# Residual sums, expert sums and gate biases accumulated in PSUM by TensorE, in a fused eight-stage metaformer kernel

## The reference, cut to what matters

```
x = x + L0_conv(ln(x))   # 7x7 neighbourhood attention
t = t + L0_ffn(ln(t))    # top 2 of 8 experts, weights softmax of the router
x = x + L1_conv(ln(x))   # 3x3 convolution by L1 distances, minus L2 distances
t = t + L1_ffn(ln(t))    # expert choice: 16 experts take 8 tokens of each image
x = x + L2_conv(ln(x))   # two deformable convolutions with batch norm between
t = t + L2_ffn(ln(t))    # top 2 of 8 experts again
x = x + L3_conv(ln(x))   # full attention, 4 heads, relative positions
t = t + L3_ffn(ln(t))    # expert choice again
```

## Time and profile before

| | us |
|---|---|
| median of 3 runs | 466.93 (466.06 to 466.94) |
| profiled execution, its own time | 465.76 |
| span of its profile, first to last instruction | 464.0 |
| PE busy / DVE busy / ACT busy / POOL busy | 399.2 / 365.1 / 272.8 / 167.3 |

### The profile page before, as it was taken

The page is one execution under the profiler, slowest core; times in us unless marked ns, Lnnn a source line. Parts: engine busy times, 40 slices in busy tenths (PEclk is TensorE's granted clock), DMA queues, the critical chain, the costliest instruction groups (busy, mean ns, idle before and its releaser), DMA issues.

```text
span 464.0 us, 10053 instructions
## 1 busy us (share of the span) xinstructions
PE 399.2 (86%) x4050; PEld 279.2 (60%) x4050; DVE 365.1 (79%) x731; ACT 272.8 (59%) x458; POOL 167.3 (36%) x158
## 2 busy tenths in 40 slices
PE   6988989989887797999878879998788996998775
PEld 5867952223246665666667556666588874554664
DVE  4778888899982577999995779999966866898521
ACT  2742177999905267887742678887412236898240
POOL 5000500000000037899982378999850500000000
PEclk9999999999999799999999999999999996999895
...
DMA packets 1630, 9.89 MB, mean 21 GB/s; under 512 B 208, under 2 KB 976, under 8 KB 1104
## 3 DMA queue, kind: packets, MB, share of 16 engines
...
...
## 4 chain that ended last, share of the span: by engine, by line
DVE 32%; PE 23%; ACT 9%; issue 6%; POOL 2%; DVEq 0%; ACTq 0%; POOLq 0%
DVE SMT L931 8%; DVE PRD L912 6%; DVE wb L912 6%; PE bank L1312 6%; ACT RINGS L605 3%; PE bank L1422 3%; PE bank L1052 2%; PE bank L1402 2%; DVE SMT L923 2%; ACT RINGS L622 1%; PE bank L1197 1%; PE bank L1295 1%; PE bank L1189 1%; ACT RINGS L547 1%; POOL HY L340 1%
## 5 line engine op out<-in xcount | busy, mean ns | idle before, releaser
L1312 PE MATMUL bank<-VB,RINGS 64*128 64x144 f32 x1152 | 95.5, 299 | 18.0 <-DVE wb L912 7.3
L1312 PEld LDWEIGHTS bank<-VB,RINGS 64*128 64x128 f32 x1152 | 76.3, 186 | 43.6 <-issue 19.6
L1052 PE MATMUL bank<-cst 128*128 128x128 f32 x650 | 79.4, 282 | 0.0
L1052 PEld LDWEIGHTS bank<-cst 128*128 128x128 f32 x650 | 78.0, 199 | 0.6
L340 POOL TENSOR_TENSOR HY<-OM,cst 128x324 f32<-128x324 f32 x32 | 23.3, 748 | 121.1 <-DVE LXA L898 121.1
L912 DVE TENSOR_TENSOR PRD<-bank,HY 128x864 f32<-128x864 f32 x48 | 50.3, 1051 | 4.7 <-PE bank L1312 4.1
L912 DVE TENSOR_TENSOR wb<-bank,HY 128x864 f32<-128x864 f32 x48 | 50.4, 1051 | 4.0 <-PE bank L1312 3.4
L547 ACT ACTIVATE RINGS<-bank,cst 128x768 f32<-128x768 f32 x48 | 42.8, 891 | 17.7 <-PE bank L1295 17.6
L550 ACT ACTIVATE RINGS<-RINGS,cst 128x768 f32<-128x768 f32 x48 | 44.9, 936 | 1.6
L1248 PE MATMUL bank<-RINGS,cst 128*32 128x512 f32 x336 | 40.7, 594 | 5.6 <-DVE RINGS L836 2.0
L501 ACT ACTIVATE RINGS<-PRD,wb 128x2048 f32<-128x2048 f32 (+1 forms) x21 | 39.5, 1920 | 5.3 <-PE bank L1248 4.3
(11 more groups left out here) (256 smaller groups left out, 701.2 us busy)
## 6 DMA issues: line engine op xcount, KB each, us to landing
...
```

What stands on the lines that cost most here:

```text
L1052: pe.matmul(bk[:, 0:P], ident, ident, start=True, stop=True)
L1312: ins = pe.matmul(view(bank[q % 2 * 2 + gp], k3 * NR, [[3 * NR, 2 * CG], [1, NR]]), view(HX, b % 2 * HXN + (3 * t + k3) * NPIX + half * P, ...
```

## The change

The two halves of every block's output now land in PSUM banks that already hold the residual: PE multiplies the identity by XT into the bank (`residual`, start without stop), and the block's last matmuls add to it. DVE's `norm` reads the sum from that bank (NORM_SRC names it); ACT copies the bank to XT after its square roots. Only norm 1 still reads XT. In `norm`, mean and centring are one instruction that reads PSUM, and the squares are ACT's. The expert matrices of the top-2 block lie by expert and then channel, and are used once per group of 32 rows instead of in a block-diagonal copy four times as wide; ACT copies the first four pairs' outputs to SBUF (EXB), all eight pairs are multiplied one after the other, POOL halves seven of them and DVE the eighth, and PE adds the remaining four terms into the bank. Router and gate biases are one-row matmuls. Expert choice picks its top 8 from the logits instead of the probabilities, so that picking and exponentials run at the same time. The tail of `deform` goes by halves, with the mean taken from SMT by matmuls. Fills are fewer before norms (223 matmuls in all instead of 325), and new ones stand between the short steps. The constants and weights are laid out to match; the weight transfers shrink.

```diff
-FILL_TAIL = 22
+FILL_TAIL = 16
 FILL_KEYS = (3, 3)
-FILL_GATES = 11
-FILL, FILL_EC = (18, 23, 40, 20, 12, 22, 40, 22), 16
+FILL_GATES, FILL_PAIR = 4, 2
+FILL, FILL_EC = (13, 18, 12, 6, 12, 9, 12, 8), 2
+FILL_HOP, FILL_PROB, FILL_DRAIN = 2, 8, 3
 GROUPS3 = 8
...
+        NORM_SRC = (twice(bank[4]), None, moe_out, halves_out, twice(bank[7]), halves_out, moe_out, twice(bank[2]))
         def cv(name, n, c=0, p0=0, np_=P):
...
+                for s in range(NT // 2 - 1):
+                    pool.wait_ge(weighed, turn * 8 + s + 1)
+                    first, last = (view(PR, s * 512 + o, [[256, 2], [1, 128]]) for o in (0, 128))
                     pool.tensor_tensor(first, first, last, ALU.add).then_inc(halved, 1)
...
+                    act.wait_ge(centred, NBH * n + bh + 1)
+                    act.activation(SQ[:, bh * NPIX:(bh + 1) * NPIX], XN[:, bh * NPIX:(bh + 1) * NPIX],
+                                   ACT.Square).then_inc(sq_made, 1)
...
+                if NORM_SRC[n] is not None:
+                    for bh in range(NBH):
+                        bk, at = NORM_SRC[n][bh]
+                        ins = act.activation(XT[:, bh * NPIX:(bh + 1) * NPIX], bk[:, at:at + NPIX], ACT.Copy)
+                    ins.then_inc(xt_kept, 1)
...
+                def keep(s):
+                    act.wait_ge(expert_done, turn * 8 + s + 1)
+                    act.activation(view(EXB, s * 512, [[1, 512]]), bank[2 + s][:, :], ACT.Copy).then_inc(expert_kept, 1)
+                keep(0)
                 act.wait_ge(gate_ready, turn + 1)
                 act.activation(EX[:, :], LG[:, :], ACT.Exp).then_inc(ex_ready, 1)
+                for s in range(1, B4):
+                    keep(s)
...
-                act.activation(PB[:, :], MK[:, :], ACT.Exp, bias=nm[:, 0:1], accum_out=rs[:, 0:1]).then_inc(ec_exp, 1)
+                act.wait_ge(ec_twice, turn + 1)
+                act.activation(PB[:, :], bank[3][:, 0:NPIX], ACT.Exp, bias=nm[:, 0:1], accum_out=rs[:, 0:1]).then_inc(ec_exp, 1)
...
-                         lambda bh: dve.tensor_scalar(one(mean, bh), one(s16, bh), 1.0 / C, None, ALU.mult),
-                         lambda bh: dve.tensor_tensor(of(SQ, bh), of(XN, bh), of(XN, bh), ALU.mult),
...
+                for bh in range(NBH):
+                    if sums is not None:
+                        dve.wait_ge(sums, first + step * bh)
+                    ins = dve.tensor_reduce(one(s16, bh), x(bh), AX.X, ALU.add)
+                    links[0] += 1
+                    ins.then_inc(dve_chain, 1)
+                for bh in range(NBH):
+                    dve.wait_ge(dve_chain, links[0] - 1 + bh)
+                    dve.scalar_tensor_tensor(of(XN, bh), per_tile(s16, bh), -1.0 / C, x(bh), ALU.mult,
+                                             ALU.add).then_inc(centred, 1)
+                for bh in range(NBH):
+                    dve.wait_ge(sq_made, NBH * n + bh + 1)
+                    dve.tensor_reduce(one(var, bh), of(SQ, bh), AX.X, ALU.add).then_inc(var_ready, 1)
...
-                    dve.tensor_tensor(view(PR, (s % 3) * 512, [[256, 2], [E8, C], [1, E8]]),
-                                      view(bank[2 + s % 4], 0, [[256, 2], [E8, C], [1, E8]]),
-                                      view(GW, (s // 4 * 8 + s % 4) * E8, [[4 * E8, 2], [0, C], [1, E8]]), ALU.mult).then_inc(expert_used, 1)
...
-                    link(dve.tensor_reduce(view(Y2, (s // 4 * 8 + s % 4) * C, [[4 * C, 2], [1, C]]),
...
-                dve.wait_ge(xt_biased, turn + 1)
-                link(dve.tensor_tensor(XT[:, :], XT[:, :], Y2[:, :], ALU.add))
+                    if s < B4:
+                        dve.wait_ge(expert_kept, turn * B4 + s + 1)
+                        outputs = view(EXB, s * 512, [[256, 2], [C, E8], [1, C]])
+                    else:
+                        dve.wait_ge(expert_done, turn * 8 + s + 1)
+                        outputs = view(bank[2 + s - B4], 0, [[256, 2], [C, E8], [1, C]])
+                    dve.tensor_tensor(view(PR, s * 512, [[256, 2], [C, E8], [1, C]]), outputs,
+                                      view(GW, (s // 4 * 8 + s % 4) * E8, [[4 * E8, 2], [1, E8], [0, C]]),
+                                      ALU.mult).then_inc(weighed, 1)
+                dve.wait_ge(weighed, turn * 8 + 8)
+                first, last = (view(PR, 7 * 512 + o, [[256, 2], [1, 128]]) for o in (0, 128))
+                dve.tensor_tensor(first, first, last, ALU.add).then_inc(last_halved, 1)
...
-                link(dve.tensor_scalar(MK[:, :], bank[1][:, 0:NPIX], w[:, at["gb"]:at["gb"] + 1], None, ALU.add))
-                link(dve.tensor_reduce(mx[:, 0:1], MK[:, :], AX.X, ALU.max))
-                dve.tensor_scalar(nm[:, 0:1], mx[:, 0:1], -1.0, None, ALU.mult).then_inc(ec_max, 1)
+                link(dve.max(top8[:, :], bank[1][:, 0:NPIX]))
+                dve.tensor_scalar(nm[:, 0:1], top8[:, 0:1], -1.0, None, ALU.mult).then_inc(ec_max, 1)
+                link(dve.match_replace(out=MK[:, :], in_to_replace=top8[:, :], in_values=bank[1][:, 0:NPIX], imm_value=NEG))
+                link(dve.tensor_scalar(MK[:, :], MK[:, :], NEG, None, ALU.is_equal))
...
+                dve.scalar_tensor_tensor(GX[:, :], PB[:, :], den[:, 0:1], MK[:, :], ALU.mult, ALU.mult).then_inc(g_ready, 1)
...
+                dve.wait_ge(mean_ready, turn + 1)
+                for bh in (1, 0):
+                    dve.wait_ge(wo_done, NBH * turn + bh + 1)
+                    if bh == 0:
+                        dve.wait_ge(sq_ready, NBH * turn + 1)
+                    dve.tensor_scalar(ACC[:, bh * NPIX:(bh + 1) * NPIX], bank[4 - 4 * bh][:, 0:NPIX], c1[:, 0:1], None,
+                                      ALU.add).then_inc(cen_ready, 1)
...
-            link(dve.tensor_tensor(tiles(XT), tiles(XT), view(wd, WD["bu1"], [[0, NT], [1, C]]), ALU.add))
-            dve.wait_ge(u_done, 1)
-            link(dve.tensor_tensor(XT[:, :], XT[:, :], bank[2][:, :], ALU.add))
...
+            def residual(bk, col, x0, n):
+                pe.matmul(bk[:, col:col + n], ident, XT[:, x0:x0 + n], start=True, stop=False, skip_group_check=True)
...
+                ones = view(cst, CST["one"], [[0, P]], n=1)
+                pe.matmul(bank[1][:, 0:P], ones, view(w, at["rb"], [[0, NT], [1, E8]], n=1), start=True, stop=False,
+                          skip_group_check=True)
...
+                def experts(bh):
                     for j in range(2):
+                        for b4 in range(B4):
+                            if bh and j == 0:
+                                pe.wait_ge(expert_kept, turn * B4 + b4 + 1)
+                            g = 2 * bh + j
+                            ins = pe.matmul(bank[2 + b4][:, j * 256:j * 256 + 256], XNC[C * b4:C * b4 + C, g * P:(g + 1) * P],
+                                            w_(w, at["ew"], 256, C * b4, C), start=True, stop=True)
+                            if j:
+                                ins.then_inc(expert_done, 1)
+                experts(0)
+                if turn:
+                    pe.wait_ge(xt_kept, 5)
+                for bh in range(NBH):
+                    residual(moe_out[bh][0], 0, bh * NPIX, NPIX)
+                experts(1)
...
+                for pair in range(4):
+                    keep_warm(bank[0], FILL_PAIR)
+                    bh, at_col = pair // 2, pair % 2 * 2 * C
+                    pe.wait_ge(halved, turn * 7 + min(2 * pair + 2, 7))
+                    if pair == 3:
+                        pe.wait_ge(last_halved, turn + 1)
+                    for e in range(E8 // 2):
+                        ins = pe.matmul(view(moe_out[bh][0], at_col, [[P, 2], [C, 2], [1, C]]), ident,
+                                        view(PR, pair * 1024 + e * C, [[256, 2], [512, 2], [1, C]]), start=False,
+                                        stop=(e == E8 // 2 - 1), skip_group_check=True)
+                    if pair % 2:
+                        ins.then_inc(mixed_done, 1)
...
-                keep_warm(bank[6], FILL_EC)
+                for bk, done in ((bank[1], ec_logits), (bank[3], ec_twice)):
+                    for bh in range(NBH):
+                        ins = pe.matmul(bk[:, 0:NPIX], w_(w, at["gw"] + bh * P), XNC[:, bh * NPIX:(bh + 1) * NPIX],
+                                        start=False, stop=(bh == NBH - 1), skip_group_check=True)
+                    ins.then_inc(done, 1)
...
+                keep_warm(bank[5], FILL_HOP)
                 pe.wait_ge(gt_ready, turn + 1)
...
+                if turn:
+                    for bh in range(NBH):
+                        pe.matmul(bank[(7, 6)[bh]][:, 0:NPIX], OB[:, bh * P:(bh + 1) * P], GX[:, :], start=False, stop=True,
+                                  skip_group_check=True).then_inc(fin_turned, 1)
...
+                def parts(bh):
+                    for g in (2 * bh, 2 * bh + 1):
+                        ins = pe.matmul(bank[5][:, 0:1], SMT[:, g * P:(g + 1) * P], cv("part", 1), start=(g == 0),
```

(22 more changed lines are left out.)

309 lines of the change are left out of this document (148 added, 161 removed).

## The result

The changed kernel takes 438.89 us (median of 4 runs, 438.81 to 443.26), the kernel before 466.5 beside it: a ratio of 0.944, 95% interval 0.939 to 0.950. The profiled execution took 438.85 us with a span of 437.1, against 465.76 and 464.0: 26.9 us less. The forecast was 437.7 us: 29.2 less than the profiled execution, and 1.17 added for the runs' median.

A forecast was written before the change was run, and what follows sets the result against it. The prediction took serial dependent chains between the overlapped loops as the bound, with no engine holding the chain. Its terms summed to 29.2 us off 465.76, giving 436.6, or 437.7 us at the runs' median; range 432 to 446.

The forecast's parts named there:

- The norm itself: All eight norms: squares and separate means leave DVE, less a 0.2 us hop to ACT; 0.65 us each, 5.2 gained.
- The rival in which ACT is late: Norms: ACT's squares and copies lose 0.5 us each; 441.7 to 444.5 us if attention fills fail too; chance 0.23.
- Additions: DVE's additions into XT go before norms: 0.72 us each before six, 4.3 in all, and 0.8 before norm 3.
- The 0.8 in this sum: Norm 0: its means took 1.12 us against norm 3's 0.29; removing them gains 0.8 more.
- The residual before the last attention's turning: Last attention: 0.9 us of residual matmuls, half covered by ACT's copy of the values; 0.4 us lost.
- Norm 7 and its product: Norm 7: fewer fills no longer outlast the work, 0.6 us; fills ahead bring the preceding product to full clock, 0.9.
- Top-2 blocks: Two top-2 blocks: new steps gain 1.1 us each with DVE and POOL excluding each other, 3.2 without; 2.1 taken.
- starts over 1 us apart: Top-2 block: sign of exclusion, second to fourth multiplication starting this far apart with POOL's halves between; 0.65 for the rival.
- Expert choice: Two expert choices: picking beside exponentials gains 2.9 us; fills holding the clock gain 1.65 in the first, 1.25 in the last.
- The end: Kernel's end: second store issued about 1.4 us after the product instead of 4.5; 3.1 us gained.
- Tails: Two deformable tails done by halves: 1.45 us gained at the first, 1.55 at the second; 3.0 together.
- Last attention: Last attention: eight fills behind the first scores shorten ACT's waits at low PE clock; 2.8 us gained, bounds 0 and 3.4.

The follow-up runs named there:

- old_steps: The changed kernel with the norms' steps of before (means as an instruction of their own, squares by a DVE multiplication): 447.94 us, ratio 0.965.
- through_xt: The changed kernel with a DVE copy to XT ahead of each norm but norm 1, in place of ACT's copies: 444.64 us, ratio 0.954.
- fewer_fills: The changed kernel with 8 fills instead of 13 in norm 0 and none ahead of the top-2 blocks' groups of sums: 439.5 us, ratio 0.944.
- residual_early: The changed kernel with the edits of psum_weights, fewer_fills and first_group_fill, and the last attention's residual products ahead of its last value group: 435.23 us.
- psum_weights: The changed kernel with the top-2 weights also written to PSUM, so four multiplications read only one SBUF operand: 440.42 us, ratio 0.944.
- no_hop_fills: The changed kernel without the fills in the gaps of the expert choices and in the last attention: 445.46 us, ratio 0.956.
- old_with_fills: The kernel before the change with only the short fills added in the expert choices and the last attention: 463.47 us, ratio 0.995.
- first_group_fill: The changed kernel with nine more fills between the first and second group of images in the last attention: 439.13 us, ratio 0.944.
- steady: residual_early without its move of the residual, with more fills around norms 1 and 5 and at the first attention's end: 434.37 us, ratio 0.933.
- steady_residual: steady with the last attention's residual products moved as in residual_early: 434.72 us, ratio 0.935.

## Why the prediction was right

It was right in the total (1.2 us off) and in nearly all its mechanisms; the terms were on the whole too high, by 2.3 us. That the total is closer than the terms is luck: the 1.17 us added for the runs' median had no counterpart in the changed kernel, whose median (438.89) is its profiled execution's time (438.85). And 1.17 of the 2.3 are one drop of the clock in the last attention, which four later profiles without more fills there don't have.

**The norm itself, 5.2.** 0.65 for each norm, as old_steps shows, except norm 0, whose fills end last: 4.6. The hop to ACT cost 0.15, forecast 0.2. The rival in which ACT is late fell: ACT waited for PE in each of the seven norms with a copy to XNC.

**Additions, 4.3 + 0.8.** 0.66 and not 0.72 or 0.8 for norms 2 to 7 (through_xt), 4.0. Norm 0 is the first step that failed, the addition together with its means and steps: 2.17 forecast, 1.62 measured, because I didn't look where the thirteen fills end. Timeline, norm 0:

```profile
5.78 3.22 PE L1055 MATMUL bank<-cst 128*128 128x128 f32 x20
8.84 0.60 PE L1067 MATMUL bank<-cst,XN 128*128 128x128 f32 x4
10.06 1.10 PE L1076 MATMUL bank<-XNC,wa 128*128 128x512 f32 x2 [0.62 <-ACT XNC L432]
```

The first scaled half was there at 7.76; PE was busy until 8.8. Before the change that half was there at 10.05, so on DVE all 2.29 us came. With eight fills they reach the next block: fewer_fills ends norm 0 at 9.26 instead of 11.54, 2.28. The 0.8 in this sum was put down to the means. old_steps shows that they are not its cause: it keeps them, and they take 0.29 us there. Before the change their 1.12 lay beside a POOL memset of 1.38 us that began at 5.83; in old_steps they are done before it. That points to the memset as the cause, which no run takes away to show it.

**The residual before the last attention's turning, −0.4.** 0.39, by residual_early, of which 0.35 reach the product.

**Norm 7 and its product, 0.6 + 0.9.** From the product to the next block 8.67 us before (434.16 to 442.83) and 5.75 now (415.60 to 421.35): 2.92, forecast 0.9 + 0.6 + 0.65 + 0.72 = 2.87.

**Top-2 blocks, 2.1.** The exclusion that I took is there, but costs half as much. I had 9.4 us for a block with it and 7.3 without; it was 8.78. The sum let three halves alternate with multiplications and charged 0.71 for each. Only two multiplications had to wait for POOL's halves, since the first two were on their way before POOL began, and each lost 0.53 (1.13 apart instead of 0.60): 1.1 and not 2.1. The row I took it from had said 0.55 too (0.94 against 0.39). The forecast's own sign, starts over 1 us apart, came at the fourth multiplication and the one behind it. The rule of the Trainium skill (page "SBUF — State Buffer", section "Who interferes with whom") is borne out in what triggers it: psum_weights takes one of DVE's inputs out of SBUF and both engines are back at their own pace. That the loser waits for the whole instruction is borne out for the most part: of a half's 0.72 us a multiplication lost 0.53, and in psum_weights VectorE's own halving, the second to start in the second block, lost 0.56 of 0.73. I had it right to price both ends. What I didn't see is that the pair fills become the bound: 1.4 to 2.3 us of PE behind everybody else in psum_weights.

**Expert choice, 2.9 + 1.65 + 1.25.** The first block gained 2.8 us from the logits to norm 4's source (16.02 before, 13.2 now), forecast 3.1; GX came 0.27 later than I had it. The last block's clock: 2.3 us are lost again when the fills go (no_hop_fills), the output product's share included.

**The end, 3.1.** From the product's start to the end of the span 6.65 us before and 3.80 now: 2.85.

**Tails, 3.0.** The first takes 6.48 us from line 923's last group (237.21) to the offsets (243.69) where it took 7.57: 1.1, forecast 1.45. The second was 0.3 short too. The scheme was right and the steps sized some 0.35 us too short.

**Last attention, 2.8.** The term that failed by most in the profile: 1.43 instead of 2.4 with the residual. Its size was right, for 56.04 became 53.42 in the profiles without a drop there, 2.6. In the changed kernel's own profile a drop behind the wait between first and second group cost 1.17, and so "a granted clock of 1.00 in ... the last attention" was wrong. That eight fills would be what gives the 2.8 is not shown. For it speaks old_with_fills, where nothing drops there and 3.0 were gained. Against it speaks no_hop_fills: without them the stretch was only 0.25 longer, and the clock was low for no longer than with them.

**Open.** What decides where a drop stands. In the expert choices the evidence for the fills is good: the clock is low there in both profiles without them (before, no_hop_fills) and at 1.00 in all twelve with them. Elsewhere no fill is shown to have stopped a drop, since kernels without it had none in the same place either; and in old_with_fills, first_group_fill, fewer_fills, steady and steady_residual one stood in stretches whose work was the same and that ran at full clock in other profiles. Single profiles can't say how often each place is hit.
